# Last attention of an audio tower: sixteen sequences to a pass, projection ahead of the turns, output product among the next round's position products

## The reference

```python
H, T, d = 8, 246, 16
P = pos_emb.shape[1]                                  # 511
q = (x @ Wq + bq).reshape(B, T, H, d)
k = (x @ Wk + bk).reshape(B, T, H, d).transpose(0, 2, 1, 3)
v = (x @ Wv + bv).reshape(B, T, H, d).transpose(0, 2, 1, 3)
p = (pos_emb @ Wp + bp).reshape(1, P, H, d).transpose(0, 2, 1, 3)
bd = rel_shift((q + pos_bias_v).transpose(0, 2, 1, 3) @ p.transpose(0, 1, 3, 2))[..., :T] / sqrt(d)
s = (q + pos_bias_u).transpose(0, 2, 1, 3) @ k.transpose(0, 1, 3, 2) / sqrt(d) + bd
out = (softmax(s) @ v).transpose(0, 2, 1, 3).reshape(B, T, H * d)
h = h + out @ Wo + bo                                 # x is the layer norm of h
```

## Time and profile before

| | us |
|---|---|
| median of 3 timed runs | 19773.57 (19770.3 to 19792.48) |
| the profiled execution | 19783.35 |
| span of its profile | 19781.6 |
| PE busy over the span | 13602.8 (69%) |
| DVE busy over the span | 10697.2 (54%) |
| ACT busy over the span | 6498.9 (33%) |
| `relative_stage`, from its first input load to the next stage's first load | 17511.15 to 19481.35, that is 1970.2 |

### The profile page before, as it was taken

The page is one execution under the profiler, slowest core; times in us unless marked ns, Lnnn a source line. Parts: engine busy times, 40 slices in busy tenths (PEclk is TensorE's granted clock), DMA queues, the critical chain, the costliest instruction groups (busy, mean ns, idle before and its releaser), DMA issues. The chain is left out here.

```text
span 19781.6 us, 591443 instructions
## 1 busy us (share of the span) xinstructions
PE 13602.8 (69%) x260405; PEld 10804.0 (55%) x260405; DVE 10697.2 (54%) x24932; ACT 6498.9 (33%) x15903; POOL 2272.5 (11%) x1398
## 2 busy tenths in 40 slices
PE   4517767775274888888888666766666665867776
PEld 3414766665252667666766445544555454745554
DVE  6431455555314555555555676767666644445555
ACT  3001234442111566665666211111111111334441
POOL 0058000000363111111111000000000000000001
PEclk9555566665675999999999677766777686977775
DMA  0313300002233111111111222022211234156663
GB/s 22 97 38 45 75 23 17 17 17 70 50 58 91 22 25 26 24 26 25 25 25 25 43 42 41 12 44 42 42 29 23 42 81 118 38 170 179 174 182 71
DMA packets 1836305, 1095.45 MB, mean 55 GB/s; under 512 B 1109402, under 2 KB 1763645, under 8 KB 1816765
## 3 DMA queue, kind: packets, MB, share of 16 engines
q1 hardware_dynamic: 1606323, 999.32, 20.9%
q0 software_dynamic: 227328, 57.19, 2.0%
HBM read 569.43 MB, written 484.53 MB: 53 GB/s over the span
## 5 line engine op out<-in xcount | busy, mean ns | idle before, releaser
L2872 PE MATMUL recur_acc<-recur_U,recur_W 8*32 8x64 f32 (+4 forms) x49152 | 1393.2, 270 | 478.8 <-ACT recur_W L2796 429.0
L2923 DVE TENSOR_TENSOR recur_pr<-recur_K,recur_e 124x64 f32<-124x64 f32 (+60 forms) x1024 | 1284.5, 1254 | 637.5 <-ACT recur_e L2808 492.3
L2872 PEld LDWEIGHTS recur_acc<-recur_U,recur_W 8*32 8x32 f32 (+4 forms) x49152 | 1065.3, 140 | 889.3 <-ACT recur_W L2796 739.1
L2859 PE MATMUL recur_acc<-recur_R,recur_E 128*32 128x64 f32 x62976 | 1195.5, 231 | 203.5 <-issue 191.9
L2928 DVE TENSOR_REDUCE recur_dot<-recur_pr 124x1 f32<-124x64 f32 (+60 forms) x1024 | 1278.8, 1249 | 21.2
L2859 PEld LDWEIGHTS recur_acc<-recur_R,recur_E 128*32 128x32 f32 x62976 | 1062.7, 117 | 308.4 <-issue 253.8
L2844 PE MATMUL recur_wT<-const_ident,recur_w 128*128 128x128 f32 (+15 forms) x1536 | 477.0, 373 | 1082.7 <-DVE recur_w L2930 1080.1
L2796 ACT ACTIVATE recur_W<-recur_wT 128x256 f32<-128x256 f32 (+16 forms) x1024 | 335.0, 327 | 2586.8 <-PE recur_wT L2844 2583.9
L2469 ACT ACTIVATE delta_B0l<-delta_pS 64x256 f32<-64x256 f32 x1968 | 743.4, 378 | 868.5 <-PE delta_pS L2369 850.6
L2469 ACT ACTIVATE delta_B1l<-delta_pS 64x256 f32<-64x256 f32 x1968 | 743.7, 378 | 704.1 <-PE delta_pS L2369 683.4
L2844 PEld LDWEIGHTS recur_wT<-const_ident,recur_w 128*128 128x128 f32 (+15 forms) x1536 | 168.2, 143 | 1251.2 <-DVE recur_w L2930 912.3
(11 more groups left out here) (613 smaller groups left out, 34773.6 us busy)
## 6 DMA issues: line engine op xcount, KB each, us to landing
scr<-rel_BD SPq DMA_DIRECT2D x128, 1288.0 KB
rel_sc<-scr SPq DMA_DIRECT2D x128, 861.0 KB
xnT<-ln_xT SPq DMA_DIRECT2D x64, 492.0 KB, 3.0
kr<-delta_QK SPq DMA_DIRECT2D x492, 64.0 KB, 2.3
ur<-delta_Uf SPq DMA_DIRECT2D x492, 64.0 KB, 2.2
zz<-delta_Z SPq DMA_DIRECT2D x492, 64.0 KB, 2.2
recur_K<-kr SPq DMA_DIRECT2D x64, 448.0 KB
recur_H<-zz SPq DMA_DIRECT2D x64, 448.0 KB
```

The costliest lines, as they stand in the source:

```text
L2859: nc.tensor.matmul(acc[a][32 * q:32 * q + 32, 0:FD], E[a][:, EQ * q + 32 * j:EQ * q + 32 * j + 32], R[a][:, m, :], start=(j == 0), stop=False)
L2872: ins = nc.tensor.matmul(acc[a][32 * q:32 * q + 32, 0:FD], W[a][0:8 * k, b, 160 * q + 32 * j:160 * q + 32 * j + 32], U[a][0:8 * k, 2 * (t ...
L2923: V.tensor_tensor(pr[0:cp, 0:n, :], K[a][0:cp, r0:r0 + n, :], e[a][0:cp, None, :].to_broadcast([cp, n, FD]), ALU.mult).then_inc(s_own[a], 1)
```

## The change

A pass takes sixteen sequences instead of eight, so the loop runs three times instead of seven, and the first and the last pass have sixteen sequences as well. `xa`, `xc` and `hb` double, and so does POOL's one instruction on `hb`. A round `j` becomes: S and B of sequence `j`, with O of sequence `j-2` put in behind the fourth B; then A, C, V of sequence `j+1`; then T and P of sequence `j-1`. DVE goes `scored` of j with `added` of j-2 behind the second of the four, `projected` of j+1, `attended` of j-1. `Vp` gets a third buffer, since the values of j+1 are now written before P of j-1 has read its own. A pass has one more, short round at its end, and SP stores the rows of h one round later. The computation is the same.

```diff
--- before.py
+++ after.py
@@ -3457,7 +3457,7 @@
 
 
     SCALE = HD ** -0.5
-    G = 8
+    G = 16
     NR = 3
     QH = NH // 2
     SCORES_AT = {0: 0, 2: 1, 5: 2, 7: 3}
@@ -3476,7 +3476,7 @@
         QV = st.sb("QV", [D, 2, T])
         QU = st.sb("QU", [D, 2, T])
         KT = st.sb("KT", [D, T])
-        Vp = [st.sb(f"Vp{k}", [HT, 2, 2, D]) for k in range(2)]
+        Vp = [st.sb(f"Vp{k}", [HT, 2, 2, D]) for k in range(3)]
         BD = [[st.sb(f"BD{k}{f}", [HT, NH, WB]) for f in range(2)] for k in range(2)]
         sc = [st.sb(f"sc{k}", [HT, 2, NH, T]) for k in range(NR)]
         PT = st.sb("PT", [HT, 2, NH, T])
@@ -3549,16 +3549,17 @@
             CU = cur is not None
             proj = lambda j: [("A", j)] * NX + [("C", j), ("V", j)] * CU
             order = proj(0)
-            for j in range(G + 1):
+            for j in range(G + 2):
                 for q in range(8 if j < G else 0):
                     order += [("S", j, SCORES_AT[q])] if CU and q in SCORES_AT else []
                     order += [("B", j, q)] * NX
-                if CU and j:
-                    order += [("T", j - 1, q) for q in range(4)] + [("P", j - 1)]
+                    order += [("O", j - 2)] * (CU and j >= 2 and q == 3)
+                if CU and j >= G:
+                    order.append(("O", j - 2))
                 if j + 1 < G:
                     order += proj(j + 1)
-                if CU and j:
-                    order.append(("O", j - 1))
+                if CU and 1 <= j <= G:
+                    order += [("T", j - 1, q) for q in range(4)] + [("P", j - 1)]
             at = {job: n for n, job in enumerate(order)}
             on_act = [job[0] in "BT" for job in order]
             act_upto = lambda *job: sum(on_act[:at[job] + 1])
@@ -3593,10 +3594,10 @@
                             if j:
                                 sp.wait_ge(s_g, at["T", j - 1, 3] + 1)
                             positions(j + 2)
-                        if CU and j:
-                            sp.wait_ge(s_dd, dve_upto("O", j - 1))
+                        if CU and j >= 2:
+                            sp.wait_ge(s_dd, dve_upto("O", j - 2))
                             for p in PARTS:
-                                sp.dma_start(rows(h_out, cur)[p, 2 * j - 2:2 * j], hb[p, 2 * j - 2:2 * j]).then_inc(s_out, 16)
+                                sp.dma_start(rows(h_out, cur)[p, 2 * j - 4:2 * j - 2], hb[p, 2 * j - 4:2 * j - 2]).then_inc(s_out, 16)
                     if NX:
                         for k in range(2):
                             sp.wait_ge(s_bw[k], 64 * (G // 2))
@@ -3675,7 +3676,7 @@
                         for k in range(4):
                             par, sh = divmod(k, 2)
                             for r in range(QH):
-                                mm(p[32 * r:32 * r + 32, 0, 0:T], Vp[j % 2][:, sh, par, 32 * r:32 * r + 32],
+                                mm(p[32 * r:32 * r + 32, 0, 0:T], Vp[j % 3][:, sh, par, 32 * r:32 * r + 32],
                                    PT[:, sh, 2 * r + par, :], k == 0, k == 3)
                             for r in range(QH):
                                 ins = mm(p[32 * r:32 * r + 32, 1, 0:T], mk[:, par, 32 * r:32 * r + 32],
@@ -3697,20 +3698,22 @@
                             values(j)
 
                     project(0)
-                    for j in range(G + 1):
+                    for j in range(G + 2):
                         for q in range(8 if j < G else 0):
                             if CU and q in SCORES_AT:
                                 scores(j, SCORES_AT[q])
                             if NX:
                                 positions(j, q)
-                        if CU and j:
+                            if CU and j >= 2 and q == 3:
+                                outs(j - 2)
+                        if CU and j >= G:
+                            outs(j - 2)
+                        if j + 1 < G:
+                            project(j + 1)
+                        if CU and 1 <= j <= G:
                             for q in range(4):
                                 turn(j - 1, q)
                             attend(j - 1)
-                        if j + 1 < G:
-                            project(j + 1)
-                        if CU and j:
-                            outs(j - 1)
 
                 @block.vector
                 def _(dve):
@@ -3731,7 +3734,7 @@
                             V.tensor_scalar(KT[:], slot("C", j)[:, 1, 0:T], cols[:, 1:2], None, ALU.add).then_inc(s_dd, 1)
                             dve.wait_ge(s_g, at["V", j] + 1)
                             four = [HT, 2, 2, D]
-                            V.tensor_tensor(Vp[j % 2][:], slot("V", j)[0:HT, 0, 0:2 * D].rearrange("p (f d) -> p f d", f=2).unsqueeze(2).to_broadcast(four),
+                            V.tensor_tensor(Vp[j % 3][:], slot("V", j)[0:HT, 0, 0:2 * D].rearrange("p (f d) -> p f d", f=2).unsqueeze(2).to_broadcast(four),
                                             mk[:, None, :, :].to_broadcast(four), ALU.mult).then_inc(s_dd, 1)
 
                     def scored(j, q):
@@ -3765,16 +3768,17 @@
                         V.tensor_tensor(hv, hv, p[0:HT, 0, 0:2 * D], ALU.add).then_inc(s_dd, 1)
 
                     projected(0)
-                    for j in range(G + 1):
-                        if CU and j < G:
-                            for q in range(4):
-                                scored(j, q)
-                        if CU and j:
-                            attended(j - 1)
+                    for j in range(G + 2):
+                        for q in range(4 if CU and j < G else 0):
+                            scored(j, q)
+                            if j >= 2 and q == 1:
+                                added(j - 2)
+                        if CU and j >= G:
+                            added(j - 2)
                         if j + 1 < G:
                             projected(j + 1)
-                        if CU and j:
-                            added(j - 1)
+                        if CU and 1 <= j <= G:
+                            attended(j - 1)
 
                 @block.gpsimd
                 def _(pool):
```

## The result

The changed kernel takes 19719.97 us (median of 13 runs, 19685.59 to 19740.17), the kernel before 19773.57 (13 runs). The ratio is 0.9969 [0.9961, 0.9978]: 54 us less. The profiled executions differ by 71.9 (spans 19709.7 and 19781.6). The prediction said 134 less.

A forecast was written before the change was run, and what follows sets the result against it. No engine is full; a chain of waits through S, turns, P and DVE's readers bounds the round. First pass 191.7, loop 1229 and last pass 415.4 make 1836 instead of 1970, 134 less: 19640 us, range 19565 to 19755.

The forecast's parts named there:

- The chain of the kernel before: Loop round: S and its readers, turns, P, reciprocal and oT 2.1 us, projections' readers 1.9 us, then S again.
- The price of the ends: First and last pass with eight more sequences each: 88 + 211 us taken back from the loop's gain.
- Rival 3: DMA takes over: rounds stay at 27.3 us if reads and stores can't exceed today's rate, 19798; chance 0.06.
- part (a): Projections ahead of the turns: new chain through DVE, T3 waiting for Vp's reader; loop round 23.8 us instead of 27.3.
- the sum's low end: Loop round of 22.7 us if the whole chain through DVE, turns and P runs at 2.4 GHz.
- Rival 1: Loop turns at 1.2 GHz, P at 2.4: 26.0 us a round, 99 more, 19739; chance 0.13.
- Part (d): Sixteen to a pass: larger loads 5.3 us where both are loaded; POOL's add some 9 us, costed at nothing.
- rival 4: Pass start: reads backlogged on SP's queue, or POOL's add meets DVE's subtract; 8 to 15 us a pass, 19685; chance 0.06.
- Rival 2: Low clock from the turns into P, loop and last pass: P 5.6 us, 28.0 a loop round, 19844; chance 0.08.

The follow-up runs named there:

- g16_only: The kernel before with sixteen sequences to a pass and nothing else: 1.0002 of the kernel before, 19812.42 us.
- inter_fill6: The changed kernel with projections interleaved among the turns and six extra matmuls behind each O of the loop: 0.9871 of the kernel before, 19511.79 us.
- fill: The changed kernel with four extra matmuls behind each O of the loop, in PE's idle time: 0.9940 of the kernel before, 19679.23 us.
- fill_v: The changed kernel with four extra matmuls right behind V, where PE has no idle time: 1.0005 of the kernel before, 19809.88 us.
- pool_split: The changed kernel with POOL's one bias add over hb cut into sixteen pieces: 0.9954 of the kernel before, 19740.78 us.

## Why the prediction was off

**Right.** The chain of the kernel before, and the direction: S behind P within 0.2 us (17815.45 beside a reciprocal at 17815.58), all gain from the order of work. The price of the ends was near: first pass 182.9 against 191.7 (the stores of sixteen sequences run on to 17683 at some 296 GB/s), last pass 399.6 against 415.4. The prediction said that fewer passes give 277 us at the present round and the ends take 299 back; g16_only measured 12 us of loss. That sentence already said that sixteen is worth nothing by itself. Rival 3 is refuted: DMA share and rate rose from 0.66 and 188 GB/s to 0.79 and 219 in inter_fill6, with no wait for a position read seen.

**The step that failed: the loop round of part (a), 23.8 against 25.40.** Over the 42 distances between reciprocals that is 67 of the 86 us by which the loop missed. The sum counted DVE's chain up to Vp and let T3 start there, at 17.0 us; it took PE to be waiting. Vp was done at 17.8 us (17832.72 and 0.68), 0.8 late, and T3 didn't start "within 0.1 us of the end of Vp" but in its turn behind T0 to T2, more than 1 us later. "A low clock among the position products, where it is now, mostly lengthens the S wait and not the turns" was true of a PE line without projections in it. The change put 3.3 us of projections (17828.82 to 17832.14 in after) into that line ahead of the turns, inside the low stretch. PE reached T0 at 16.6, and P began at 21.4, in the longer rounds at 22.5, instead of 19.1 by the sum's low end and 20.2 by the 23.8 taken. DVE's idle time ahead of the reciprocal, forecast at some 6 us, was 7.13 and 8.24. The sum of PE's own work from the fifth position product on was never made; fill and fill_v show it was the bound, from both sides. QU, too, waited 0.30 us for C, where the prediction had the DVE chain run through.

**Rival 1** had almost the size (26.0 a round, 19739) and the wrong place: it put the low clock into the turns behind DVE readers; it lay mostly in the work ahead of them, and in every second round also in the first turns (4.58 us instead of 3.60). That the number came near is luck.

**Part (d), loads.** PE starts on the second load 4.84 us behind the first (17686.53 to 17691.37), where it was 2.66 with loads of half the size. POOL's add was to come at 12 to 21 us of round 1 and cost nothing. It came at some 8 (17718.25, where that sequence's Vp had started at 17710.34): counted from PE's first A it came 31.7 us in instead of 25.7, 6 later and not the 14 forecast. There it met a DVE instruction that the prediction had not on its list, the small scaling: 3 us a pass, by pool_split, the lesser form of what rival 4 had priced at 8 to 15. Its other half, a backlog of reads, didn't come: no wait for a read of positions stands in the loop of after. The remaining 10 of the 86 us are not explained.

**The last pass** was forecast at 25.4 a round and took 23.68; settled, its rounds are 23.89 in after as in before. P did start late, 20.3 us behind the reciprocal (19202.23 to 19222.53; forecast 20.8), but it ran at the high clock, 0.62 us for eight records instead of 1.05: 3.6 us instead of the 5.6 assumed. Rival 2, the low clock kept into P, therefore fell in the loop and in the last pass. The two windows of after, last pass:

```profile
19212.00:19221.10 9.10, 8.19 (x36) 7.44 (x36) 6.22 (x9) 2.98 (x3) 0.00 (x0) 0.50 0.00 0
19221.30:19226.00 4.70, 3.57 (x67) 2.39 (x66) 0.00 (x0) 4.56 (x8) 0.00 (x0) 1.00 0.78 181
```

From 19212.88 on PE did nothing but transposes, and the clock rose inside the last sixteen of them, before P. The rule of the Trainium skill that the prediction weighed ("TensorE: Matmul & The Clock Gate", Part 4: PE-mode transpose), that transposes don't count as PE work for the clock, disagrees with this trace of float32 transposes.

**From 134 to 54.** In the profile, the stage gives 72: the loop 86 short, the ends 25 better, which hides a part of the loop's miss. Between the profiled pair (71.9) and the medians (54) lie 18 us more. Both profiled executions are single runs, before's 9.8 above its median and after's 8.5 below, and after's 13 runs spread over 55 us: this part comes from which executions were profiled.

## What to carry over

Before moving work into the gap ahead of a wait, add up what the engine itself does up to that point, at the clock of that stretch: an engine that is busy 9.5 of 10.1 us has no gap. A move out of one chain can be a move into another, and two moves may be worth something only together; take the change apart before crediting a part. Where a short wait is followed by a low clock, a few matmuls with no reader in that wait can be worth more than any reordering, and reordering that brought nothing may pay once the clock is high.

## What was unexpected of the hardware

- Six idle-time matmuls a round (2.65 us) held the clock at 1.00 for all the rounds of a pass (in its first loop pass from 17735 to 18049); in fill four held it for three whole rounds, 0.94 in the mean. Loop rounds: 25.40 without, 21.89 with six and interleaving.
- With the idle time in place the rounds alternate between 24.95 and 26.05, and so does the place of the low stretch, from 6.1 or from 8.5 us of the round on. What moves it, these runs don't show.
- Rounds settle at the same length in kernels with different orders: 27.31 in the loops of before, g16_only and fill_v, 23.89 in the last passes of before, g16_only, after and fill_v. Each of them has one low stretch of the clock, at the same place in every round. Why, these runs don't show, but a microsecond of work put in or taken out need not show as one in the round.
- One POOL instruction of 9.28 us over SBUF held a DVE instruction over four elements a partition for 6.39 us, and DVE with it; at 4.53 us of POOL it held a larger one 4.90. The Trainium skill ("SBUF — State Buffer", section "SBUF: two separate sides") says that the port pair shared by the two is locked for a whole instruction by the one that starts first; the trace agrees, and with sixteen shorter instructions (11.95 us together in pool_split) the loop is 9 us shorter.
